# A depthwise stage's tables with memory of their own, made ready while x loads

## The chip, the cores and the metric

The kernel runs on one core of a Trainium2 chip. The metric is the device time of one execution in microseconds (us); the times given are medians over several executions.

## The reference, cut to what matters

x is [128, 256, 9, 9] in float32: 128 images, 256 channels, 81 pixels. One block is computed: a normalisation over channels, a convolutional attention, and a mixture of eight experts behind it. Cut to the parts around the change:

```python
xn = _ln_c(x)                                  # mean and variance over the 256 channels of each pixel
k  = xn.reshape(bs, c, hw).transpose(0, 2, 1)
k1 = conv1d(k, se_key_w, groups=hw) + se_key_b # 9 taps along the channels, a filter for each pixel
v  = conv2d(xn, se_val_w, groups=c) + se_val_b # 3x3 depthwise
k1s = relu(bn(conv2d(xn, sa_key_w, groups=c))) # 3x3 depthwise, with a batch norm folded in
out1 = band of softmax weights over v, + k1
out2 = k1s + softmax(...) * xn
x = x + alpha * out1 + (1 - alpha) * out2
x = x + experts(_ln_t(x))                      # top 2 of 8 experts on 10368 tokens
```

## The kernel before, in words

Five engines run programs of their own, written out by hand and joined by semaphores; SP issues nearly all DMAs, on one queue, in the order of its program. Two large buffers in on-chip memory, `big` and `pool_`, hold 128 partitions (images) by 20736 words each; a third, `aux`, has 4640 words. Parts of `pool_` and `aux` are handed out anew in each stage, by a cursor that is set back.

**Load and statistics.** SP issues the two halves of x into `big` (L264), twenty small weight loads (L273), and then one store from memory to memory that lays out the windows of the 1-D convolution, `u_d`, 81 x 128 rows of 544 bytes (L278); it waits for that. VectorE takes statistics of each pixel (L741, 60 pixels as two halves, 21 whole), with its sums after them (L756 to L763), one root on ScalarE (L1218) and a reciprocal (L731).

**Pixel stage, 27 turns of three pixels.** ScalarE normalises (L1226), POOL copies the result back to `big` (L1418), TensorE transposes (L426), VectorE copies the transposes to `xt_s` (L772), and TensorE convolves them with windows that SP loads from `u_d` into one of two buffers (L284, issued when the convolution of the turn before last is done); VectorE adds the bias and writes k1 over all of `pool_` (L781).

**Between the stages.** Once all of k1 is in `pool_`, its first columns must be stored to memory before the tables can lie there: SP stores words 0 to `tables_end` (5147) of 128 rows (L291) and waits; then it issues three small tables (L295: taps, batch norm and rows, 11 partitions each), the mask (L296: 75 partitions, 973 KB) and the rest of k1's first half (L297). VectorE meanwhile makes se_ab, sa_ab and alpha (L794 to L800), waits for the tables, folds the batch norm into the taps with a root on ScalarE (L804, L1240) and splits them into three bf16 parts (L803 to L816). Then it waits for the store of L297 and for POOL, and a memset of `pt_s` (L819) releases TensorE, POOL and ScalarE through `tab_c`.

**Depthwise stage, eight chunks of 32 channels.** VectorE copies the chunk's taps (L822). TensorE builds 82 x 162 matrices, one for each channel, as mask times taps (L475, nine groups of nine matmuls); ScalarE (L1248) and VectorE (L828) copy them in turn into `m_s`, which lies in `pool_` behind the tables. Then for eight quads of channels POOL copies xn (L1431), TensorE turns it (L459) and multiplies it by the matrices (L493), VectorE and ScalarE evict (L834, L1257, L1259), and SP stores v and ks (L310). The stores of xn (L302) and of k1's second half (L304) are issued between them.

Behind it come the attention stage, the router and the experts, which the change does not touch.

The lines that order the pause:

```python
            sp.wait_ge(S["k1_ev"], PIX_TURNS + CREDIT)
            sp.dma_start(k1_d[:, 0:tables_end], pool_[:, 0:tables_end]).then_inc(S["k1_out0"], 16)
            sp.wait_ge(S["k1_out0"], 16)
...
            dve.wait_ge(S["k1_outm"], 16)
            dve.wait_ge(S["xb_c"], PIX_TURNS + CREDIT)
            nc.vector.memset(pt_s[:, :, :, :], 1.0).then_inc(S["tab_c"], 1)
```

Of the kernel before, what the change touches and what calls it, by code (L numbers as in the profile page):

```python
# [4 lines left out]
BS, C, H, W = 128, 256, 9, 9  # L5
HW = H * W
# [6 lines left out]
BN_EPS, LN_C_EPS, LN_T_EPS = 1e-5, 1e-6, 1e-5  # L13
# [12 lines left out]
QUADS = C // QUAD  # L26
DEPTH = 4
CHUNK = 32
AUX = 4640
TAP_ROWS = 64 + 11  # L30
PIECE = 512
PIECES = EXPERTS * 4
# [18 lines left out]
def metaformer_kernel(nc, x, taps, tap_bn, tap_rows, toeplitz_mask, ident, band_masks, rot_masks, zstrings,  # L51
# [10 lines left out]
    fp32, fp16, bf16 = mybir.dt.float32, mybir.dt.float16, mybir.dt.bfloat16  # L62
    ALU, ACT, AX = mybir.AluOpType, mybir.ActivationFunctionType, mybir.AxisListType

    ctx = ExitStack()
    with ctx:
# [44 lines left out]
        cursor = [0]  # L111

        def take(parts, *dims):
            n = 1
            for d in dims:
                n *= d
            a = pool_[0:parts, cursor[0]:cursor[0] + n]
            cursor[0] += n
            assert cursor[0] <= C * HW
            names = "abcde"[:len(dims)]  # L120
            if len(dims) > 1:
                a = a.rearrange(f"p ({' '.join(names)}) -> p {' '.join(names)}",
                                **{m: d for m, d in zip(names, dims)})
            return a
# [23 lines left out]
        xt_s = take_aux(128, 2, PIX, C)  # L148
        kb_s = take_aux(128, HW)

        ps = ctx.enter_context(nc.psum_tensor("ps", [128, 8, 512], fp32))


        cursor[0] = 0
        bn_s = take(128, HW, 2 * HALVES, 3)

        cursor[0] = 0
        mask_s = take(TAP_ROWS, HW * (HW + 1) // 2).bitcast(bf16).rearrange("p (m n) -> p m n", n=HW + 1)
        taps_s = take(11, 2, C)
        tapr_s = take(11, 2, C)  # L160
        taph_s = take(TAP_ROWS, C).bitcast(bf16).rearrange("p (v c) -> p v c", v=2)
        tapc_s = take(TAP_ROWS, CHUNK).bitcast(bf16).rearrange("p (v c) -> p v c", v=2)
        tapbn_s = take(11, 2, C)
        taprow_s = take(11, 2)
        tables_end = cursor[0]
        m_s = take(HW + 1, CHUNK, 2, HW)
        assert cursor[0] <= C * HW // 2
        aux_at[0] = 0
        xq_s = take_aux(128, 2, QUAD, HW)
        pt_s = take_aux(HW + 1, 2, QUAD, BS)  # L170
# [89 lines left out]
        @block.sync  # L260
        def _(sp):
            half = C * HW // 2
            for h in range(HALVES):
                sp.dma_start(big[:, h * half:(h + 1) * half], x[:, h * half:(h + 1) * half]).then_inc(S[f"x_in{h}"], 16)  # L264
            n = 0
# [8 lines left out]
                n += 1  # L274
            assert 16 * n == W_IN

            window = bass.AP(zstrings.tensor, 127, [[ZLEN, HW], [-1, 128], [1, 136]])
            sp.dma_start(u_d, window).then_inc(S["win_out"], 16)  # L278
            sp.wait_ge(S["win_out"], 16)
# [8 lines left out]
                    load_bands(i * 2 + par, par)  # L288
            load_bands(PIX_TURNS - 1, 0)
            sp.wait_ge(S["k1_ev"], PIX_TURNS + CREDIT)  # L290
            sp.dma_start(k1_d[:, 0:tables_end], pool_[:, 0:tables_end]).then_inc(S["k1_out0"], 16)  # L291
            sp.wait_ge(S["k1_out0"], 16)

            for dst, src in ((taps_s, taps), (tapbn_s, tap_bn), (taprow_s, tap_rows)):
                sp.dma_start(dst, src).then_inc(S["tab_in"], 16)  # L295
            sp.dma_start(mask_s.bitcast(mybir.dt.uint16), toeplitz_mask).then_inc(S["mask_in"], 16)  # L296
            sp.dma_start(k1_d[:, tables_end:half], pool_[:, tables_end:half]).then_inc(S["k1_outm"], 16)  # L297
            sp.wait_ge(S["xb_c"], PIX_TURNS + CREDIT)
            with sp.Fori(0, QUADS // DEPTH) as i:

# [12 lines left out]
            for k in range(DEPTH):  # L313
                sp.wait_ge(S[f"st_v{k}"], 32 * (QUADS // DEPTH) + CREDIT)
            sp.wait_ge(S["xn_out"], 16 * (QUADS // DEPTH))
            sp.wait_ge(S["k1_out1"], 16 * (QUADS // DEPTH))

            def load_pair(i, first=False):
# [391 lines left out]
        def _(dve):  # L710
# [10 lines left out]
            def link(ins):  # L721

                start(ins)
                settled()
# [7 lines left out]

            early, unroll = 60, 15

            def pixel_statistics(first, pixels, run, chans, part):
# [56 lines left out]
            for p, ab in ((se_bn_s[:, :].unsqueeze(1), se_ab[:, :].unsqueeze(1)), (sa_bn_s, sa_ab)):  # L794
# [4 lines left out]
                link(nc.vector.tensor_tensor(ab[:, :, 1:2], bb, ab[:, :, 2:3], ALU.subtract))  # L799
            link(nc.vector.tensor_scalar(alpha_s[:, 1:2], alpha_s[:, 0:1], -1.0, 1.0, ALU.mult, ALU.add))  # L800

            dve.wait_ge(S["tab_in"], 48)
            link(nc.vector.memset(taph_s, 0.0))  # L803
            inverse_root(tapbn_s[:, 1, :], BN_EPS, 1.0, tapbn_s[:, 1, :])  # L804
            link(nc.vector.tensor_tensor(tapbn_s[:, 0, :], tapbn_s[:, 0, :], tapbn_s[:, 1, :], ALU.mult))
            link(nc.vector.tensor_scalar(tapbn_s[:, 0, :], tapbn_s[:, 0, :], taprow_s[:, 0:1], taprow_s[:, 1:2],
                                         ALU.mult, ALU.add))
            link(nc.vector.tensor_tensor(taps_s[:, 1, :], taps_s[:, 1, :], tapbn_s[:, 0, :], ALU.mult))


            for k in range(3):
                part = taph_s[32 * k:32 * k + 11]
                left = taps_s if k == 0 else tapr_s
                link(nc.vector.tensor_copy(part, left))
                if k < 2:
                    link(nc.vector.tensor_tensor(tapr_s, left, part, ALU.subtract))  # L816
            dve.wait_ge(S["k1_outm"], 16)
            dve.wait_ge(S["xb_c"], PIX_TURNS + CREDIT)
            nc.vector.memset(pt_s[:, :, :, :], 1.0).then_inc(S["tab_c"], 1)  # L819
            with dve.Fori(0, C // CHUNK) as i:  # L820
                dve.wait_ge(S["mb_p"], i * 9 + CREDIT)
                nc.vector.tensor_copy(tapc_s[:, :, :], taph_s[:, :, bass.ds(i * CHUNK, CHUNK)]).then_inc(S["tapc_c"], 1)  # L822
                for n in range(1, 9, 2):
                    dve.wait_ge(S["mb_p"], i * 9 + n + 1 + CREDIT)
                    if n == 1:
                        dve.wait_ge(S["cv_p"], i * 8 + CREDIT)
                    flat = ps[0:HW + 1, 2:4, :].rearrange("p b n -> p (b n)")[:, 0:9 * 2 * CHUNK]
                    nc.vector.tensor_copy(m_s[:, :, :, n * 9:(n + 1) * 9].rearrange("p c v m -> p m v c"),  # L828
                                          flat.rearrange("p (m v c) -> p m v c", m=9, v=2)).then_inc(S["mb_e1"], 1)
                for k in range(CHUNK // QUAD):  # L830
                    q, par = i * (CHUNK // QUAD) + k, k % 2
                    dve.wait_ge(S["tq_p"], q + 1 + CREDIT)
                    dve.wait_ge(S["cv_p"], q - 1 + CREDIT)
                    nc.vector.tensor_copy(pt_s[0:HW, par, :, :].rearrange("p c b -> p (c b)"),  # L834
                                          ps[0:HW, 4 + par, :]).then_inc(S["pt_c"], 1)
# [379 lines left out]
        @block.scalar  # L1215
        def _(act):
            act.wait_ge(S["var_c"], 1)
            nc.scalar.activation(stats[:, 1, :], stats[:, 1, :], ACT.Sqrt).then_inc(S["root_c"], 1)  # L1218

            def normalise(i, par):  # L1220
# [12 lines left out]
                    normalise(i * 2 + par, par)  # L1233
            normalise(PIX_TURNS - 1, 0)
            for n, v in enumerate((se_ab[:, 0:1], sa_ab[:, :, 0:1])):
                act.wait_ge(S["var_c"], n + 2)
                nc.scalar.activation(v, v, ACT.Sqrt).then_inc(S["root_c"], 1)

            act.wait_ge(S["var_c"], 4)
            nc.scalar.activation(tapbn_s[:, 1, :], tapbn_s[:, 1, :], ACT.Sqrt).then_inc(S["root_c"], 1)  # L1240
            act.wait_ge(S["tab_c"], 1)
            with act.Fori(0, C // CHUNK) as i:
                for n in range(0, 9, 2):
                    act.wait_ge(S["mb_p"], i * 9 + n + 1 + CREDIT)
# [332 lines left out]
```

## Time and profile before

| | |
|---|---|
| time, three runs | 1769.7, 1773.2, 1778.4 us (median 1773.2) |
| the profiled execution, its own time | 1770.6 us |
| its span, first to last instruction | 1768.9 us |
| TensorE matmul busy | 1377.7 us (78%) |
| VectorE busy | 1140.3 us (64%) |
| ScalarE busy | 802.4 us (45%) |
| GpSimd busy | 650.0 us (37%) |
| moved by DMA | 250.5 MB |

In the rows, PE is TensorE's matmuls, PEld its weight loads, DVE VectorE, ACT ScalarE, POOL GpSimd, SP SyncE; SPq is SP's sequencer, which issues the DMAs. L with a number is a line of the kernel. Busy times of overlapping engines do not add up to the span; idle time of an engine costs only where the chain of waits runs through it.

### The profile page before, as it was taken

How to read it: one execution, taken by the hardware profiler on the slowest of the kernel's cores; microseconds unless marked ns; L12 is line 12 of the kernel's file. 1: busy time of each engine (PE TensorE's matmuls, PEld its weight loads, DVE VectorE, ACT ScalarE, POOL GpSimd, SP SyncE). 2: the span in 40 equal slices, each digit the busy share in tenths (PEclk: the TensorE clock that was granted, in tenths of full speed). 3: DMA queues.
4: the chain of work that ended last, by engine and by line, in shares of the span. 5: the costliest groups of instructions: out<-in, count | busy, mean ns of one | idle time of the engine just before them, and what ended most of it. 6: DMA issues, size and time to landing. Idle time of an engine off the chain costs nothing.

```text
span 1768.9 us, 38225 instructions
## 1 busy us (share of the span) xinstructions
PE 1377.7 (78%) x9764; PEld 1124.1 (64%) x9765; DVE 1140.3 (64%) x3074; ACT 802.4 (45%) x1779; POOL 650.0 (37%) x561
## 2 busy tenths in 40 slices
PE   0393988979999999999755555399999999999300
PEld 0383888955666666666555555288888888888300
DVE  6894343326767666676478888566666666666493
ACT  0491444435434344444299999233333333333250
POOL 0260111114333333333056767354544545445200
PEclk9995888879999999999555555699999999999755
DMA  8534435468666666765133333432323223332485
GB/s 300 122 91 170 183 149 194 166 188 190 159 169 155 160 162 153 173 150 142 50 99 122 125 122 123 144 92 81 95 85 94 85 88 92 87 94 76 177 317 240
DMA packets 259222, 250.50 MB, mean 142 GB/s; under 512 B 150089, under 2 KB 234398, under 8 KB 255156
## 3 DMA queue, kind: packets, MB, share of 16 engines
q1 hardware_dynamic: 238879, 196.95, 38.0%
q0 software_dynamic: 20320, 53.28, 9.1%
q8 instruction: 9, 0.15, 0.0%
q14 instruction: 14, 0.11, 0.0%
HBM read 152.07 MB, written 105.57 MB: 146 GB/s over the span
## 4 chain that ended last, share of the span: by engine, by line
PE 68%; DVE 12%; ACT 7%; DMA 6%; issue 4%; SPq 1%; DVEq 1%; ACTq 0%; POOLq 0%; POOL 0%
PE ps L686 14%; PE ps L671 13%; PE ps L510 6%; PE ps L493 5%; PE ps L459 4%; PE ps L565 3%; PE ps L537 3%; PE ps L561 3%; ACT pool_ L1248 2%; PE ps L520 2%; PE ps L655 2%; DVE big L1205 2%; PE ps L529 2%; PE ps L563 2%; DMA aux<-u_d 2%
## 5 line engine op out<-in xcount | busy, mean ns | idle before, releaser
L1475 POOL DMA_INDIRECT y_d<-pool_,to_s x176 | 254.8, 1447 | 282.8 <-DVE pool_ L1165 246.8
L686 PE MATMUL ps<-pool_,aux 128*128 x2112 | 249.6, 274 | 5.2 <-DVE aux L1157 3.4
L671 PE MATMUL ps<-aux,pool_ 128*128 128x256 f16 x2112 | 246.8, 274 | 1.0 <-ACT aux L1376 0.6
L686 PEld LDWEIGHTS ps<-pool_,aux 128*128 128x128 f16 x2112 | 198.4, 98 | 50.5 <-issue 23.5
L671 PEld LDWEIGHTS ps<-aux,pool_ 128*128 x2112 | 206.5, 98 | 25.9 <-issue 1.6
L1376 ACT ACTIVATE aux<-ps,b_s 128x256 f32<-128x256 f32 x352 | 138.0, 474 | 162.2 <-DVE aux L1157 162.0
L1455 POOL DMA_INDIRECT rows_d<-aux,idx_s x162 | 160.2, 989 | 108.3 <-DVE idx_s L1068 58.9
L1165 DVE SCALAR_TENSOR_TENSOR pool_<-ps,pool_ 128x512 f32<-128x512 f32 x88 | 60.9, 692 | 140.0 <-PE ps L686 140.0
L1447 POOL DMA_DIRECT2D pool_<-v_d x64 | 50.0, 781 | 272.4 <-PE ps L567 271.0
L1368 ACT ACTIVATE aux<-ps 128x512 f16<-128x512 f32 x88 | 52.6, 597 | 172.7 <-PE ps L655 172.7
L510 PE MATMUL ps<-pool_,se_w_s 81*81 81x512 f32 x256 | 118.7, 607 | 5.6 <-DMA pool_<-k_d 5.6
L1283 ACT ACTIVATE pool_<-ps,sa_ab 128x324 f32<-128x324 f32 x64 | 39.7, 621 | 159.7 <-PE ps L522 159.7
L1157 DVE TENSOR_TENSOR aux<-aux 128x1024 f16<-128x1024 f32 x88 | 107.8, 1225 | 3.1
L1431 POOL COPY aux<-big 128x324 f32 x64 | 29.2, 457 | 215.6 <-PE ps L459 186.3
L834 DVE COPY aux<-ps 81x512 f32<-81x512 f32 x64 | 43.9, 686 | 87.5 <-PE ps L459 87.5
L459 PE MATMUL ps<-ident_s,aux 128*81 128x128 f32 x512 | 77.9, 302 | 25.7 <-POOL aux L1431 25.7
L1295 ACT ACTIVATE pool_<-ps,pool_ 128x81 f32<-128x81 f32 x256 | 79.5, 336 | 29.2 <-DVE pool_ L865 29.2
L855 DVE TENSOR_REDUCE pool_<-ps 128x4 f32<-128x324 f32 x64 | 31.6, 496 | 93.5 <-PE ps L529 91.9
L493 PE MATMUL ps<-pool_,aux 82*128 82x162 f32 x512 | 90.5, 326 | 0.0
L459 PEld LDWEIGHTS ps<-ident_s,aux 128*81 128x81 f32 x512 | 70.7, 173 | 25.9 <-POOL aux L1431 25.9
L493 PEld LDWEIGHTS ps<-pool_,aux 82*128 82x128 f32 x512 | 81.4, 209 | 0.6
L426 PE MATMUL ps<-ident_s,aux 128*128 128x128 f32 x162 | 23.5, 284 | 70.6 <-ACT aux L1226 70.6
(202 smaller groups left out, 3079.2 us busy)
## 6 DMA issues: line engine op xcount, KB each, us to landing
pool_<-rows_d SPq DMA_DIRECT2D x88, 258.0 KB
pool_<-y_d SPq DMA_DIRECT2D x18, 1152.0 KB, 8.7
big<-in_x SPq DMA_DIRECT2D x2, 5184.0 KB, 21.0
xn_d<-big SPq DMA_DIRECT2D x16, 648.0 KB, 3.0
v_d<-aux SPq DMA_DIRECT2D x64, 162.0 KB, 1.9
ks_d<-aux SPq DMA_DIRECT2D x64, 162.0 KB, 2.0
pool_<-xn_d SPq DMA_DIRECT2D x32, 324.0 KB
pool_<-k_d SPq DMA_DIRECT2D x32, 324.0 KB
```

The source lines that it names most:

```text
L459: last = nc.tensor.matmul(ps[0:HW, 4 + par, c * BS:(c + 1) * BS], xq_s[:, par, c, :], ident_s[:, :], start=True, stop=True)
L493: last = nc.tensor.matmul(o, pt_s[:, par, c, :], m_s[:, k * QUAD + c, :, :] .rearrange("p v n -> p (v n)"), start=True, stop=True)
L510: last = nc.tensor.matmul(ps[0:HW, n, :], se_w1_s[:, k, :], kq_s[:, par, k, 2 * n:2 * n + 2, :].rearrange("p b j -> p (b j)"), start=k == ...
L537: last = nc.tensor.matmul(ps[:, 2, TOK + j * D:TOK + (j + 1) * D], a_s[:, par, j // 2, (j % 2) * 128:(j % 2 + 1) * 128], se_w2_s[:, :], st ...
L671: last = nc.tensor.matmul(o, w_s[:, a, bass.ds(e * (4 * PIECE) + (k * HID + j * 128), 128)], xh_s[:, par, b, k * SLOTS:(k + 1) * SLOTS], s ...
L686: last = nc.tensor.matmul(ps[:, 6 + par, s * C:(s + 1) * C], hh_s[:, par, a, j, s * 128:(s + 1) * 128], w_s[:, b, bass.ds(e * (4 * PIECE) ...
L1157: nc.vector.tensor_tensor(lo, hf_s, hi, ALU.subtract).then_inc(S["hlo_c"], 1)
L1165: nc.vector.scalar_tensor_tensor(yo_s[:, par], ps[:, 6 + par, :].rearrange("p (s c) -> p s c", s=2), 1.0 / WSCALE, b2_s[:, bass.ds(e * C, ...
L1295: ins = nc.scalar.activation(e_s[:, par, h, b, :], ps[:, 2 + h, b * HW:(b + 1) * HW], ACT.Exp, bias=sm_s[:, par, 2, j:j + 1], accum_out=sm ...
L1376: nc.scalar.activation(hf_s[:, j * SLOTS:(j + 1) * SLOTS], ps[:, 2 + 2 * par + j // 2, (j % 2) * SLOTS:(j % 2 + 1) * SLOTS], ACT.Gelu, bia ...
L1455: nc.gpsimd.indirect_dma_start(out=rows_d[:, :], out_offset=bass.IndirectOffsetOnAxis(ap=idx_s[:, slot, k:k + 1], axis=0), in_=xf_s[:, slo ...
L1475: nc.gpsimd.indirect_dma_start(out=y_d[:, :], out_offset=bass.IndirectOffsetOnAxis(ap=to_s[:, par, k:k + 1], axis=0), in_=yo_s[:, par, k, ...
```

## The change

The mask (`mask_s`), the split taps (`taph_s`) and a chunk's taps (`tapc_s`) move from `pool_` to the end of `aux`, which grows from 4640 to 7904 words. The tables that the split reads go to the second half of `pool_`. SP issues the three tables ahead of x, and the mask between the weights and the window store. VectorE folds and splits the taps ahead of its statistics; ScalarE's root for it comes first. The matrices `m_s` now begin at word 0 of `pool_`. SP stores their 5184 words of rows 0 to 95 first, then those of rows 96 to 127, then the rest of the half, with no wait between; VectorE's and ScalarE's first matrix copies wait for the store of 96 rows, the memset no longer waits for a store.

```diff
--- before.py
+++ after.py
@@ -26,7 +26,7 @@
 QUADS = C // QUAD
 DEPTH = 4
 CHUNK = 32
-AUX = 4640
+AUX = 7904
 TAP_ROWS = 64 + 11
 PIECE = 512
 PIECES = EXPERTS * 4
@@ -148,23 +148,27 @@
         xt_s = take_aux(128, 2, PIX, C)
         kb_s = take_aux(128, HW)

+        mask_s = take_aux(TAP_ROWS, HW * (HW + 1) // 2).bitcast(bf16).rearrange("p (m n) -> p m n", n=HW + 1)
+        taph_s = take_aux(TAP_ROWS, C).bitcast(bf16).rearrange("p (v c) -> p v c", v=2)
+        tapc_s = take_aux(TAP_ROWS, CHUNK).bitcast(bf16).rearrange("p (v c) -> p v c", v=2)
         ps = ctx.enter_context(nc.psum_tensor("ps", [128, 8, 512], fp32))


         cursor[0] = 0
         bn_s = take(128, HW, 2 * HALVES, 3)

-        cursor[0] = 0
-        mask_s = take(TAP_ROWS, HW * (HW + 1) // 2).bitcast(bf16).rearrange("p (m n) -> p m n", n=HW + 1)
+        cursor[0] = C * HW // 2
         taps_s = take(11, 2, C)
         tapr_s = take(11, 2, C)
-        taph_s = take(TAP_ROWS, C).bitcast(bf16).rearrange("p (v c) -> p v c", v=2)
-        tapc_s = take(TAP_ROWS, CHUNK).bitcast(bf16).rearrange("p (v c) -> p v c", v=2)
         tapbn_s = take(11, 2, C)
         taprow_s = take(11, 2)
-        tables_end = cursor[0]
+        cursor[0] = 0
         m_s = take(HW + 1, CHUNK, 2, HW)
-        assert cursor[0] <= C * HW // 2
+        m_end = cursor[0]
+        m_rows = 96
         aux_at[0] = 0
         xq_s = take_aux(128, 2, QUAD, HW)
         pt_s = take_aux(HW + 1, 2, QUAD, BS)
@@ -260,6 +264,8 @@
         @block.sync
         def _(sp):
             half = C * HW // 2
+            for dst, src in ((taps_s, taps), (tapbn_s, tap_bn), (taprow_s, tap_rows)):
+                sp.dma_start(dst, src).then_inc(S["tab_in"], 16)
             for h in range(HALVES):
                 sp.dma_start(big[:, h * half:(h + 1) * half], x[:, h * half:(h + 1) * half]).then_inc(S[f"x_in{h}"], 16)
             n = 0
@@ -274,6 +280,7 @@
                 n += 1
             assert 16 * n == W_IN

+            sp.dma_start(mask_s.bitcast(mybir.dt.uint16), toeplitz_mask).then_inc(S["mask_in"], 16)
             window = bass.AP(zstrings.tensor, 127, [[ZLEN, HW], [-1, 128], [1, 136]])
             sp.dma_start(u_d, window).then_inc(S["win_out"], 16)
             sp.wait_ge(S["win_out"], 16)
@@ -288,13 +295,9 @@
                     load_bands(i * 2 + par, par)
             load_bands(PIX_TURNS - 1, 0)
             sp.wait_ge(S["k1_ev"], PIX_TURNS + CREDIT)
-            sp.dma_start(k1_d[:, 0:tables_end], pool_[:, 0:tables_end]).then_inc(S["k1_out0"], 16)
-            sp.wait_ge(S["k1_out0"], 16)
-
-            for dst, src in ((taps_s, taps), (tapbn_s, tap_bn), (taprow_s, tap_rows)):
-                sp.dma_start(dst, src).then_inc(S["tab_in"], 16)
-            sp.dma_start(mask_s.bitcast(mybir.dt.uint16), toeplitz_mask).then_inc(S["mask_in"], 16)
-            sp.dma_start(k1_d[:, tables_end:half], pool_[:, tables_end:half]).then_inc(S["k1_outm"], 16)
+            sp.dma_start(k1_d[0:m_rows, 0:m_end], pool_[0:m_rows, 0:m_end]).then_inc(S["k1_out0"], 16)
+            sp.dma_start(k1_d[m_rows:BS, 0:m_end], pool_[m_rows:BS, 0:m_end]).then_inc(S["k1_outm"], 16)
+            sp.dma_start(k1_d[:, m_end:half], pool_[:, m_end:half]).then_inc(S["k1_outm"], 16)
             sp.wait_ge(S["xb_c"], PIX_TURNS + CREDIT)
             with sp.Fori(0, QUADS // DEPTH) as i:

@@ -313,6 +316,7 @@
             for k in range(DEPTH):
                 sp.wait_ge(S[f"st_v{k}"], 32 * (QUADS // DEPTH) + CREDIT)
             sp.wait_ge(S["xn_out"], 16 * (QUADS // DEPTH))
+            sp.wait_ge(S["k1_outm"], 32)
             sp.wait_ge(S["k1_out1"], 16 * (QUADS // DEPTH))

             def load_pair(i, first=False):
@@ -732,6 +736,22 @@

+            dve.wait_ge(S["tab_in"], 48)
+            link(nc.vector.memset(taph_s, 0.0))
+            inverse_root(tapbn_s[:, 1, :], BN_EPS, 1.0, tapbn_s[:, 1, :])
+            link(nc.vector.tensor_tensor(tapbn_s[:, 0, :], tapbn_s[:, 0, :], tapbn_s[:, 1, :], ALU.mult))
+            link(nc.vector.tensor_scalar(tapbn_s[:, 0, :], tapbn_s[:, 0, :], taprow_s[:, 0:1], taprow_s[:, 1:2],
+                                         ALU.mult, ALU.add))
+            link(nc.vector.tensor_tensor(taps_s[:, 1, :], taps_s[:, 1, :], tapbn_s[:, 0, :], ALU.mult))
+            for k in range(3):
+                part = taph_s[32 * k:32 * k + 11]
+                left = taps_s if k == 0 else tapr_s
+                link(nc.vector.tensor_copy(part, left))
+                if k < 2:
+                    link(nc.vector.tensor_tensor(tapr_s, left, part, ALU.subtract))
             early, unroll = 60, 15

             def pixel_statistics(first, pixels, run, chans, part):
@@ -799,22 +819,6 @@
                 link(nc.vector.tensor_tensor(ab[:, :, 1:2], bb, ab[:, :, 2:3], ALU.subtract))
             link(nc.vector.tensor_scalar(alpha_s[:, 1:2], alpha_s[:, 0:1], -1.0, 1.0, ALU.mult, ALU.add))

-            dve.wait_ge(S["tab_in"], 48)
-            link(nc.vector.memset(taph_s, 0.0))
-            inverse_root(tapbn_s[:, 1, :], BN_EPS, 1.0, tapbn_s[:, 1, :])
-            link(nc.vector.tensor_tensor(tapbn_s[:, 0, :], tapbn_s[:, 0, :], tapbn_s[:, 1, :], ALU.mult))
-            link(nc.vector.tensor_scalar(tapbn_s[:, 0, :], tapbn_s[:, 0, :], taprow_s[:, 0:1], taprow_s[:, 1:2],
-                                         ALU.mult, ALU.add))
-            link(nc.vector.tensor_tensor(taps_s[:, 1, :], taps_s[:, 1, :], tapbn_s[:, 0, :], ALU.mult))
-
-
-            for k in range(3):
-                part = taph_s[32 * k:32 * k + 11]
-                left = taps_s if k == 0 else tapr_s
-                link(nc.vector.tensor_copy(part, left))
-                if k < 2:
-                    link(nc.vector.tensor_tensor(tapr_s, left, part, ALU.subtract))
-            dve.wait_ge(S["k1_outm"], 16)
             dve.wait_ge(S["xb_c"], PIX_TURNS + CREDIT)
             nc.vector.memset(pt_s[:, :, :, :], 1.0).then_inc(S["tab_c"], 1)
             with dve.Fori(0, C // CHUNK) as i:
@@ -822,6 +826,8 @@
                 nc.vector.tensor_copy(tapc_s[:, :, :], taph_s[:, :, bass.ds(i * CHUNK, CHUNK)]).then_inc(S["tapc_c"], 1)
                 for n in range(1, 9, 2):
                     dve.wait_ge(S["mb_p"], i * 9 + n + 1 + CREDIT)
+                    if n == 1:
+                        dve.wait_ge(S["k1_out0"], 16)
                     if n == 1:
                         dve.wait_ge(S["cv_p"], i * 8 + CREDIT)
                     flat = ps[0:HW + 1, 2:4, :].rearrange("p b n -> p (b n)")[:, 0:9 * 2 * CHUNK]
@@ -1215,6 +1221,8 @@
         @block.scalar
         def _(act):
             act.wait_ge(S["var_c"], 1)
+            nc.scalar.activation(tapbn_s[:, 1, :], tapbn_s[:, 1, :], ACT.Sqrt).then_inc(S["root_c"], 1)
+            act.wait_ge(S["var_c"], 2)
             nc.scalar.activation(stats[:, 1, :], stats[:, 1, :], ACT.Sqrt).then_inc(S["root_c"], 1)

             def normalise(i, par):
@@ -1233,12 +1241,11 @@
                     normalise(i * 2 + par, par)
             normalise(PIX_TURNS - 1, 0)
             for n, v in enumerate((se_ab[:, 0:1], sa_ab[:, :, 0:1])):
-                act.wait_ge(S["var_c"], n + 2)
+                act.wait_ge(S["var_c"], n + 3)
                 nc.scalar.activation(v, v, ACT.Sqrt).then_inc(S["root_c"], 1)

-            act.wait_ge(S["var_c"], 4)
-            nc.scalar.activation(tapbn_s[:, 1, :], tapbn_s[:, 1, :], ACT.Sqrt).then_inc(S["root_c"], 1)
             act.wait_ge(S["tab_c"], 1)
+            act.wait_ge(S["k1_out0"], 16)
             with act.Fori(0, C // CHUNK) as i:
                 for n in range(0, 9, 2):
                     act.wait_ge(S["mb_p"], i * 9 + n + 1 + CREDIT)
```

## Rows read from the trace of the kernel before

**Rows 1.** The page's part 4: the chain that ended last, by line.
```profile
PE ps L686 14%; PE ps L671 13%; PE ps L510 6%; PE ps L493 5%; PE ps L459 4%; PE ps L565 3%; PE ps L537 3%; PE ps L561 3%; ACT pool_ L1248 2%; PE ps L520 2%; PE ps L655 2%; DVE big L1205 2%; PE ps L529 2%; PE ps L563 2%; DMA aux<-u_d 2%
```

**Rows 2.** Stage table: busy us by engine, granted clock, DMA share, GB/s.
```profile
core 0: us, PE busy (x) PEld busy (x) DVE busy (x) ACT busy (x) POOL busy (x), PEclk, DMA share, GB/s
137.00:161.00 24.00, 0.00 (x0) 0.00 (x0) 8.73 (x25) 0.82 (x3) 0.37 (x1) 0.56 0.83 306
```

**Rows 3.** Chain of waits, 128 to 230 us: start, us, what.
```profile
137.06 7.59 DMA k_d<-pool_
...
146.22 12.76 DMA k_d<-pool_
...
163.87 1.26 ACT pool_ L1248
```

**Rows 4.** Timeline, 128 to 190 us, VectorE: start, us, instruction, idle before and releaser.
```profile
139.32 0.15 DVE L800 TENSOR_SCALAR alpha_s<-alpha_s 128x1 f32<-128x1 f32 x1
...
147.05 0.27 DVE L803 MEMSET pool_<- 75x256 uint32 x1 [7.58 <-DMA pool_<-in_tap_rows]
...
153.57 0.42 DVE L814 CAST pool_<-pool_ 11x512 bf16<-11x512 f32 x1
159.29 0.91 DVE L819 MEMSET aux<- 82x1024 f32 x1 [5.30 <-DMA k_d<-pool_]
```

**Rows 5.** Timeline, 0 to 100 us, SP's issues, VectorE and TensorE.
```profile
0.84 0.86 SPq L264 DMA_DIRECT2D big<-in_x  x2
...
16.25 44.63 DVE L741 BATCH_NORM_STATS2 pool_<-big  x141 [16.12 <-DMA big<-in_x]
...
31.45 1.01 SPq L278 DMA_DIRECT2D u_d<-in_zstrings  x1
...
70.41 29.12 SPq L284 DMA_DIRECT2D aux<-u_d  x13
...
72.16 1.54 PE L426 MATMUL ps<-ident_s,aux 128*128 128x128 f32 x6 [0.62 <-ACT aux L1226]
...
73.49 0.78 PE L437 MATMUL ps<-aux 128*128 128x132 f32 x2
```

**Rows 6.** Chain of waits, 60 to 130 us: a window load.
```profile
76.12 2.69 DMA aux<-u_d
```

**Rows 7.** DMA issues by line: count, KB each, median us to landing.
```profile
big<-in_x SPq DMA_DIRECT2D x2, 5184.0 KB, 21.0
...
aux<-u_d SPq DMA_DIRECT2D x27, 204.0 KB, 2.6
...
k_d<-pool_ SPq DMA_DIRECT2D x1, 2573.5 KB, 7.6
...
pool_<-in_toeplitz_mask SPq DMA_DIRECT2D x1, 972.9 KB, 7.2
```

**Rows 8.** Stage table: window store, mask and second k1 store under way.
```profile
38.00:40.00 2.00, 0.00 (x0) 0.00 (x0) 2.00 (x9) 0.00 (x0) 0.00 (x0) 1.00 0.67 164
...
150.00:151.00 1.00, 0.00 (x0) 0.00 (x0) 0.93 (x3) 0.00 (x0) 0.00 (x0) 0.50 0.87 207
...
155.00:156.00 1.00, 0.00 (x0) 0.00 (x0) 0.00 (x0) 0.00 (x0) 0.00 (x0) 0.50 1.08 464
```

**Rows 9.** Stage table: granted clock 5 us after the last matmul.
```profile
140.00:141.00 1.00, 0.00 (x0) 0.00 (x0) 0.00 (x0) 0.00 (x0) 0.00 (x0) 0.55 0.77 329
```

**Rows 10.** Chain of waits, 128 to 230 us: matmuls and transposes of one quad.
```profile
174.30 2.23 PE ps L493 x8
...
185.97 1.11 PE ps L493 x8
187.08 0.88 PE ps L459 x8
```

**Rows 11.** Timeline, 160 to 400 us: VectorE's tap copy that begins a chunk.
```profile
188.63 0.18 DVE L822 COPY pool_<-pool_ 75x64 bf16 x1
217.74 0.18 DVE L822 COPY pool_<-pool_ 75x64 bf16 x1
244.15 0.17 DVE L822 COPY pool_<-pool_ 75x64 bf16 x1
```

## The prediction, made before the changed kernel was run

> **What bounds the kernel now.** I read the page's chain first. TensorE heads it with the two expert matmul lines, and the pixel stage's window loads have 2% [rows 1]: no engine's share tells what this change is worth, so I went to the two places that it touches. The table of stages shows the larger one: from 137 to 161 us TensorE does nothing, VectorE has 8.7 us of work, and the DMA engines are 83% busy [rows 2]. The chain there says why [rows 3]: the last k1 column is in at 137.06; the first store of k1 takes 7.59 us and SP waits for it; 1.6 us go to issuing tables and mask; the second store then takes 12.76 us, and VectorE stands before its memset (L819) until 159.29. The matrices' first copy by ScalarE (L1248) starts at 163.87. Beside that, VectorE ends its small constants at 139.47 and idles until the tables are in at 147.05, where its tap split runs 6.94 us, to 153.99 [rows 4]. The split is thus covered by the second store, and moving it alone is worth nothing.
>
> The other place is the start. SP issues x at 0.84, the window store at 31.45 and, once that has landed, the first window load at 70.41. The statistics run without a gap from 16.25 to 60.88; the first convolution starts at 73.49, right behind the second group of transposes [rows 5]. From there every second turn waits for a window load, issued when the convolution before last is done: 2.69 us, then the convolution [rows 6]. What delays the first load delays all 27 turns by as much.
>
> **The change, part by part.** All times are those of the profiled execution: span 1768.9, own time 1770.6; the median of the runs is 1773.2, 2.6 above it. A measurement of this kernel can tell about 0.5%, 8.9 us, from no change.
>
> *The pause.* Removed from the path: the wait for the whole store, the issue of tables and mask, the second store, the split. VectorE reaches the memset right behind its last constant, at 139.5 (POOL's copies back to big went turn by turn, and I count them done). The same steps as before follow: memset, POOL's copy, TensorE's first quad, nine mask matmuls, together 163.87 − 159.29 = 4.58 us from memset to first copy [rows 3, 4], so that copy could start at 144.1. It now waits for the 96-row store as well. That one is issued at 137.06 and is three quarters of a store that took 7.59 us [rows 3, 7]: by bytes, with 1.6 us of it fixed (estimated from the 1.6 us between the last table's issue and its landing, [rows 4]), 6.1 us, so there would be nothing to wait for. The nearest row for a transfer with fewer than 128 rows speaks against bytes: the mask, 75 rows, moved at 207 GB/s with the engines 87% busy, where a store of 128 rows went at 464 GB/s [rows 8], and its 0.97 MB took 7.2 us to land [rows 7]. So I take the full 7.6 us: landed at 144.65, and the first copy at 144.75. The upper bound is the 12.8 us of the store that had the mask ahead and others behind: 149.9. Gain: 163.87 − 144.75 = 19.1 us (bounds 19.8 and 14.0).
>
> A rule of the Trainium skill bears on this, "SBUF — State Buffer", section "Door 1: The DMA port swizzle": partitions 0 to 63 reach only eight of the sixteen ports. By it 96 rows last as long as 128 and the gain is 19.1; by bytes alone it would be 19.8. The mask's row agrees with the rule.
>
> The clock was granted at half (1.2 of 2.4 GHz) within 5 us of the last matmul [rows 9]; with matmuls resuming at 141.4 instead of 161.1 it has fallen too, so the first chunk is priced as it is. The rest of k1's first half, then xn and the first part of the second half, follow on the same queue: 6.3 MB in all, at 464 GB/s 13.6 us, over near 151, before the first v store is due. Waits in the loops that are already met I count at nothing: the semaphore is full from the first chunk on.
>
> *The split at the start.* Three tables are issued ahead of x. At 0.43 us each (two issues of x took 0.86 [rows 5]) x starts 1.3 us later and lands at 17.4 instead of 16.1. Tables land some 1.6 us after their issue, so at 3.6; the split's 6.94 us end at 10.5. Cover: x's load, 6.9 us of it spare; without that each us would count. ScalarE's root lies in the 6.94. Price on VectorE's chain 1.3 us, and the same for everything that SP issues later.
>
> *The mask ahead of the window store.* Here the change gives back. The mask's issue puts another 0.4 us before the window store, and its packets stand in front of that store's in the same queue. It landed after 7.2 us [rows 7]; without some 2 us of start and landing, the engines have it for 5 to 5.5 us. If the window store's packets had room beside it, the cost would be nil: that store ran with 67% of the engines busy. But the mask kept them 87% busy for only 207 GB/s [rows 8], so I take them one after the other. The window store starts 1.3 + 0.4 + 5 = 6.7 us later, less some 0.4 where the issue overlaps: 6.3; it is bound by its own 10,368 rows of 544 bytes, so it ends as much later. The first load was issued at 70.41 and takes 2.6 [rows 5, 7], so it was in at 73.0 to 73.1, 0.4 us before it was needed: 5.9. The first convolution and the step to the next load took 73.49 to 76.12 on its slow first matmuls and may win up to 1 us with its inputs all there; I take 0.4 off. **5.5 us later.** Bounds: 1.3 (the mask wholly beside the rest, VectorE's chain alone) and 1.3 + 0.4 + 7.2 − 0.3 = 8.6.
>
> *Sum:* −19.1 + 5.5 = −13.6 us: 1770.6 becomes 1757.0, and at the level of the median 1759.6. I say 1759.
>
> **The rivals.** *A, the mask is hidden* (chance 0.17): the window store leaves a third of the engines' time free, and 1 MB is little beside 38 us of it. Against: the queue is one, and the mask stands in front. Gain 19.1 − 1.3 = 17.8: 1755.5.
>
> *B, the first store lands late* (0.12): two more stores, 3.3 MB, and then xn are issued right behind it without a wait. The row for it is the second store, 12.8 us for 2.6 MB with neighbours; against it, x's halves landed one after the other (the first in by 16.1, the median of the two 21.0 [rows 5, 7]), so the queue keeps its order well. First copy at 149.9: 14.0 − 5.5 = 8.5: 1764.7, at the border of no change.
>
> *C, the granted clock* (0.09, of which 0.03 slower). Place: each of the eight chunks. It begins at the half clock, which rises in its dense half, at times sooner, at times later: from 188.63 to 217.74 a chunk took 29.1 us, the next 26.4 [rows 11]. If the shift puts six more chunks at the price of the first, some 2 us each, 12 us go: 1771.2, the same. Price at the worst: eight matmuls of L493 took 2.23 us at the half clock, 1.11 at the full one, and eight transposes 0.88 at the full one [rows 10], so if the rise never comes inside a chunk, its eight quads cost 8 × (1.12 + 0.88) = 16 us more, less some 3 already paid: 8 × 13 = 104, and the time is some 1863, slower. It decides from 13.6 + 8.9 = 22.5 us over the eight chunks, 2.8 us each. Against: the code of a chunk is unchanged, and nothing makes TensorE's work in it thinner.
>
> *D, the wait is not gone* (0.04): the tables land only when x has, whose rows of 41 KB follow in the same queue. x's halves land at 17.4 and, by the median of the two, at 28.3; then the split ends at 35.2, the statistics start 19 us late, and all is given back: 1773. It decides from tables landing after 10.5. Against: they are issued first and are 45 KB.
>
> **How the numbers follow.** Forecast as worked, 0.58: faster by over 0.5%. A, 0.17: faster. B, 0.12: around the border, 0.07 faster, 0.05 same. C, 0.09: 0.06 same, 0.03 slower. D, 0.04: 0.03 same, 0.01 slower. Together faster 0.82, same 0.14, slower 0.04. The range goes from A with the first chunks losing some 4 us less on the clock than they did, 1773.2 − 17.8 − 4 = 1751.4, to B with the mask at its upper bound, 1773.2 − (14.0 − 8.6) = 1767.8.
>
> **What would show it.** In the changed kernel: the split between 3.6 and 11 us, statistics from 17.5; the first window load issued at 76 to 77 and the first convolution at 79; k1 in at 142.6; the memset at 145; the 96-row store landing 7.6 us after its issue; ScalarE's first copy 7.7 us after k1 is in, instead of 26.8; chunks of 27 to 29 us behind it. It is wrong if the first window load is issued before 74 (A), if that first copy waits for the store by over 3 us (B), if the chunks together last over 8 us longer (C), or if the statistics start after 20 (D).

## The result, and the profile after

| | before | changed |
|---|---|---|
| median of 5 runs | 1773.2 us | 1761.4 us (1759.0 to 1763.4) |
| ratio, 95% interval | | 0.9921 [0.9898, 0.9945] |
| profiled execution, own time | 1770.6 us | 1759.0 us |
| its span | 1768.9 us | 1757.3 us |

The kernel is faster by 0.8%, 11.6 us between the two spans. The forecast was 1759, within 1751 to 1768. Measured twice more beside other kernels, the changed kernel stood at 0.9924 [0.9909, 0.9938] and 0.9936 [0.9918, 0.9953] of the kernel before, 13.2 and 12.4 us between the medians.

The span of each falls into four stretches whose edges are rows: k1 in (issue of its first store), first matrix copy by ScalarE, last chunk's tap copy, end.

| stretch | before | changed | difference |
|---|---|---|---|
| start to k1 in | 137.06 | 144.00 | +6.94 |
| k1 in to first copy | 26.81 | 9.21 | −17.60 |
| first copy to last chunk's tap copy | 188.93 | 187.73 | −1.20 |
| from there to the end | 1416.1 | 1416.4 | +0.3 |

The change touches the first two stretches. Together they gave back 10.7 us; the last 0.9 of the 11.6 lie in stretches that it does not touch.

The timeline of the changed kernel, 0 to 85 us, answers to [rows 5] (columns as there):

```profile
3.24 0.27 DVE L740 MEMSET aux<- 75x256 uint32 x1 [3.11 <-DMA pool_<-in_tap_rows]
...
9.74 0.42 DVE L751 CAST aux<-pool_ 11x512 bf16<-11x512 f32 x1
17.98 44.62 DVE L761 BATCH_NORM_STATS2 pool_<-big  x141 [7.82 <-DMA big<-in_x]
...
32.95 0.44 SPq L283 DMA_DIRECT2D aux<-in_toeplitz_mask  x1
33.43 1.01 SPq L285 DMA_DIRECT2D u_d<-in_zstrings  x1
...
73.86 1.54 PE L430 MATMUL ps<-ident_s,aux 128*128 128x128 f32 x6 [0.62 <-ACT aux L1234]
```

The split runs from 3.24 to 10.16 and VectorE then idles 7.82 us, waiting for x: the split is free here. The window store is issued 2.0 us later than before. Its landing shows in the chain of waits, 60 to 100 us (start, us, what), which answers to [rows 6]:

```profile
33.43 42.17 DMA u_d<-in_zstrings
...
75.97 2.64 DMA aux<-u_d
...
78.83 0.81 PE ps L441 x2
79.64 0.44 PE ps L443 x2
...
81.84 1.28 PE ps L430 x6
...
84.29 0.23 PE ps L443 x2
...
94.12 0.66 PE ps L430 x6
```

The chain now runs through the store itself, for 42.2 us; before, from 31.45 to 70.05, it took 38.6. The first convolution comes at 78.83, 5.3 us later, and it waits for the window load, no longer for the transposes. A pair of its matmuls takes 0.44 us, twice the 0.23 of later, and they stay slow until 84.0, where before they were quick from 75.3 on. TensorE had stood from 75.4 to 78.83, but it had not been quick before that either: six transposes (L430) took 1.54 us at 73.86, and on the chain six take 1.28 us at 81.84 and 0.66 at 94.12. The stage table prints a granted clock of 1.00 over all of this. That is a gap and not a reading: the trace's first record of the granted clock is the one of full speed that begins at 84.0 in this trace and at 75.3 in the one before, and where there is no record the table prints 1.00. The durations and the first record agree.

The pause, in the timeline of 142 to 154 us, answers to [rows 3, 4]:

```profile
144.00 0.36 SPq L298 DMA_DIRECT2D k_d<-pool_  x1
...
146.27 0.15 DVE L820 TENSOR_SCALAR alpha_s<-alpha_s 128x1 f32<-128x1 f32 x1
146.69 0.91 DVE L823 MEMSET aux<- 82x1024 f32 x1 [0.28 <-DVE alpha_s L820]
...
148.54 2.00 PE L463 MATMUL ps<-ident_s,aux 128*81 128x128 f32 x8 [6.12 <-POOL aux L1438]
...
153.09 1.23 DVE L834 COPY pool_<-ps 82x576 f32<-82x576 f32 x1 [5.45 <-DMA k_d<-pool_]
153.21 1.24 ACT L1255 ACTIVATE pool_<-ps 82x576 f32<-82x576 f32 x1 [7.77 <-DMA k_d<-pool_]
```

The memset stands right behind VectorE's constants, and both first copies wait for the store of 96 rows. The DMA issues by line (count, KB each, us to landing) answer to [rows 7]:

```profile
k_d<-pool_ SPq DMA_DIRECT2D x1, 2592.0 KB, 19.6
...
k_d<-pool_ SPq DMA_DIRECT2D x1, 1944.0 KB, 8.9
...
aux<-in_toeplitz_mask SPq DMA_DIRECT2D x1, 972.9 KB, 7.5
k_d<-pool_ SPq DMA_DIRECT2D x1, 648.0 KB, 13.9
```

The 96-row store has a quarter fewer bytes than the store before and needs 1.3 us more from issue to landing, 8.9 for 7.6. The rest of the half takes 19.6 us, and nobody waits for it.

### The profile page after: what moved, and what is told of

It is laid out like the page before. It is cut to its first block, busy times and chain, and to the rows that moved or that the text cites. A ratio compares the mean times of both kernels' runs of the same rounds, so it can differ in the third digit from the quotient of the medians.

```text
span 1757.3 us, 38235 instructions
## 1 busy us (share of the span) xinstructions
PE 1375.9 (78%) x9764; PEld 1122.8 (64%) x9765; DVE 1140.7 (65%) x3074; ACT 802.5 (46%) x1779; POOL 649.3 (37%) x561
## 4 chain that ended last, share of the span: by engine, by line
PE 68%; DVE 11%; ACT 7%; DMA 6%; issue 3%; SPq 3%; DVEq 0%; ACTq 0%; POOLq 0%; POOL 0%
PE ps L690 14%; PE ps L675 13%; PE ps L514 6%; PE ps L497 5%; PE ps L463 4%; PE ps L541 3%; PE ps L569 3%; PE ps L565 2%; DMA u_d<-in_zstrings 2%; ACT pool_ L1255 2%; PE ps L524 2%; PE ps L659 2%; DVE big L1211 2%; PE ps L533 2%; PE ps L567 2%
## 5 line engine op out<-in xcount | busy, mean ns | idle before, releaser
L675 PEld LDWEIGHTS ps<-aux,pool_ 128*128 x2112 | 206.3, 98 | 25.4 <-issue 1.5
L430 PE MATMUL ps<-ident_s,aux 128*128 128x128 f32 x162 | 24.2, 290 | 72.3 <-ACT aux L1234 72.3
L1425 POOL COPY big<-aux 128x768 f32 (+1 forms) x27 | 42.1, 1557 | 95.6 <-ACT aux L1234 95.6
```

The source lines that it names most:

```text
L675: last = nc.tensor.matmul(o, w_s[:, a, bass.ds(e * (4 * PIECE) + (k * HID + j * 128), 128)], xh_s[:, par, b, k * SLOTS:(k + 1) * SLOTS], s ...
```

## The experiments

Each is the changed kernel with one edit. A single span of this kernel moves by some us in stretches that no edit touches: over all kernels here the one from first copy to the last chunk's tap copy took 186.8 to 190.8 us, the one behind it 1416 to 1424. The first of these follows TensorE's clock: in the fourteen traces the granted clock was at half for 73.2 to 78.7 us of it, least where the stretch was shortest and most where it was longest. So edits of a few us are read from the stretch they touch. The first four kernels were run once each, and so was the kernel before, at 1775.6.

**The wait restored.** Tables and mask stay early, but the memset waits for all of k1's first half:

```diff
+            dve.wait_ge(S["k1_outm"], 32)
             dve.wait_ge(S["xb_c"], PIX_TURNS + CREDIT)
             nc.vector.memset(pt_s[:, :, :, :], 1.0).then_inc(S["tab_c"], 1)
```

> The changed kernel, but VectorE's memset waits for all of k1's first half again, as in the kernel before; tables and mask stay early. Theory (the gain of the change is the wait, not the split or the mask): the last of the three stores landed 19.6 us after its issue in the changed kernel, so the memset comes near 164.5 and the first copy near 169, 25 us after k1 is in: 16 us slower than the changed kernel, 1775. Rival (the early tables and mask brought the gain): under 5 us slower.

1777.4 us, and the timeline shows VectorE before the memset:

```profile
142.74 0.36 SPq L298 DMA_DIRECT2D k_d<-pool_  x1
...
163.58 0.91 DVE L824 MEMSET aux<- 82x1024 f32 x1 [18.43 <-DMA k_d<-pool_]
...
168.17 1.25 ACT L1256 ACTIVATE pool_<-ps 82x576 f32<-82x576 f32 x1 [24.00 <-PE ps L479]
```

25.4 us from k1 in to the first copy, as expected, against 26.8 in the kernel before: of the 17.6 us that the change took out of this stretch, 16.2 are back, and the whole advantage over the kernel before is gone. The gain is the wait; the early tables and mask only make it possible.

**The split behind the pixel stage again.** The tables need memory of their own for it, in aux:

```diff
-            dve.wait_ge(S["tab_in"], 48)
-            link(nc.vector.memset(taph_s, 0.0))
...
             link(nc.vector.tensor_scalar(alpha_s[:, 1:2], alpha_s[:, 0:1], -1.0, 1.0, ALU.mult, ALU.add))
+            dve.wait_ge(S["tab_in"], 48)
+            link(nc.vector.memset(taph_s, 0.0))
...
```

> The changed kernel, but the tables lie in aux and VectorE folds and splits the taps behind the pixel stage again, between its constants and the memset. Theory (the split had to move because the store that covered it is gone): its 6.9 us now stand on the path behind k1, the memset 6.9 us later than in the changed kernel, the first matrix copy about 11.6 + 2.5 = 14.1 us after k1 is in instead of 9.2, the kernel 4.9 us slower than the changed one. Rival (the store of 96 rows covers it still): first copy 9.2 us after k1, no difference.

k1 was in at 142.81 and the first copy came at 157.12, released by TensorE and not by the store:

```profile
152.53 0.91 DVE L822 MEMSET aux<- 82x1024 f32 x1 [0.28 <-DVE aux L816]
...
157.12 1.25 ACT L1254 ACTIVATE pool_<-ps 82x576 f32<-82x576 f32 x1 [10.74 <-PE ps L478]
```

14.3 us for 9.2: without its cover the split costs 5.1 of its 6.9 us, the rest being the time that the store takes anyway. Here the copy comes 4.59 us behind the memset, with no store in its way. 1766.6 us.

**The neighbours held back.**

```diff
             sp.dma_start(k1_d[0:m_rows, 0:m_end], pool_[0:m_rows, 0:m_end]).then_inc(S["k1_out0"], 16)
+            sp.wait_ge(S["k1_out0"], 16)
             sp.dma_start(k1_d[m_rows:BS, 0:m_end], pool_[m_rows:BS, 0:m_end]).then_inc(S["k1_outm"], 16)
```

> The changed kernel, but SP waits for the store of 96 rows before it issues the next stores. Theory (the neighbours behind it in the queue slow it): it lands after 7.6 us instead of 8.9 and the first matrix copy comes 7.9 us after k1, a gain of 1.3 us. Rival (96 rows are slow by themselves, through the rows that they lie in): it lands after 8.9 us as before and nothing moves. Rival (bytes alone): 6.1 us, the first copy then bound by the mask matmuls, 7.1 us after k1.

```profile
k_d<-pool_ SPq DMA_DIRECT2D x1, 1944.0 KB, 8.8
```

8.8 us with nothing behind it, the first copy 9.1 us after k1. So the neighbours are not the cause. That it is not the bytes either, but the rows that the store takes, the next runs show. The whole took 1764.3 us, which says nothing: the copy's gain is 0.1 us, the stretch behind the chunks was 1423.

**All 128 rows in one store.**

```diff
-        m_rows = 96
+        m_rows = BS
...
-            sp.dma_start(k1_d[m_rows:BS, 0:m_end], pool_[m_rows:BS, 0:m_end]).then_inc(S["k1_outm"], 16)
...
-            sp.wait_ge(S["k1_outm"], 32)
+            sp.wait_ge(S["k1_outm"], 16)
```

> The changed kernel, but one store takes all 128 rows of the matrices' words and the first copies wait for it; the store of 32 rows goes. Theory (the 96 rows are held up by the rows 0 to 63 and their neighbours, not by their number): it lands after the same 8.9 us, within 0.5. Rival (bytes count): 8.9 us grow by a third of the part that is not fixed, to 11.3 us, and the first copy comes 2.4 us later. Rival (the split store costs a fixed part of its own): it lands earlier, 7.6 us, as the whole store did before.

The chain of waits, 142 to 182 us:

```profile
142.03 7.64 DMA k_d<-pool_
...
149.99 1.25 ACT pool_ L1254
```

A third more bytes land 1.2 us earlier, after 7.6 us, as the whole store did before the change. The first copy comes 7.96 us behind k1, right behind the store, and VectorE's first copy waits for TensorE. The kernel ran at 1766.1 us, with 1424 in the stretch behind the chunks. The expectation's last rival gave this time. The stage tables of the two, in 1 us steps, show how the rows went (last column GB/s, the one before it the DMA engines' busy share). A row of 20.7 KB counts whole, with its bytes and its time, in the step in which it starts: 332 GB/s are sixteen rows, 664 are two waves of sixteen and no rate of the engines, and a share can exceed 1. Held back, 96 rows:

```profile
145.00:146.00 1.00, 0.00 (x0) 0.00 (x0) 0.89 (x2) 0.00 (x0) 0.00 (x0) 0.50 0.57 187
146.00:147.00 1.00, 0.21 (x1) 0.21 (x2) 0.00 (x0) 0.00 (x0) 0.72 (x2) 0.50 1.11 353
147.00:148.00 1.00, 1.00 (x6) 1.00 (x6) 0.00 (x0) 0.00 (x0) 0.13 (x1) 0.50 0.84 311
148.00:149.00 1.00, 1.00 (x10) 0.98 (x9) 0.00 (x0) 0.00 (x0) 0.00 (x0) 0.50 0.71 270
149.00:150.00 1.00, 1.00 (x15) 0.89 (x13) 0.00 (x0) 0.00 (x0) 0.46 (x1) 0.50 0.31 99
```

128 rows in one:

```profile
144.00:145.00 1.00, 0.00 (x0) 0.00 (x0) 0.66 (x4) 0.00 (x0) 0.00 (x0) 0.50 0.80 332
145.00:146.00 1.00, 0.00 (x0) 0.00 (x0) 0.67 (x2) 0.00 (x0) 0.00 (x0) 0.50 0.77 332
146.00:147.00 1.00, 0.43 (x2) 0.43 (x3) 0.00 (x0) 0.00 (x0) 0.86 (x2) 0.50 1.56 664
147.00:148.00 1.00, 1.00 (x7) 1.00 (x6) 0.00 (x0) 0.00 (x0) 0.00 (x0) 0.50 0.77 332
148.00:149.00 1.00, 1.00 (x13) 0.98 (x12) 0.00 (x0) 0.00 (x0) 0.18 (x1) 0.50 0.77 332
```

The 96 rows run unevenly and thin out at the end; the 128 run in even waves. The trace's records of single rows say the same more sharply. Each of the 128 rows took 0.77 to 0.81 us, and the sixteen parts of the store's completion came within 0.2 us, 7.44 to 7.65 behind the issue. Of the 96 rows, held back, 31 took 1.2 to 1.9 us and the others mostly 0.8, and the parts came from 6.3 to 8.8. The first row starts 0.86 to 0.87 us behind the issue in both, and the rows' times add up to about the same, 98.9 us for 96 and 100.3 for 128. So the expectation's reason, a fixed part for the split, is not what happened: the lost time lies in single slow rows. What makes those rows slow these records do not show.

**112 rows**, the same line with 112, run once later (the kernel before then stood at 1773.9, median of eleven):

> The changed kernel with 112 rows in the first store instead of 96 (7 for each of 16 engines instead of 6). 128 rows landed in 7.6 us, 96 in 8.8 to 8.9. Theory (any share of the rows that leaves the ports uneven is slow): it lands after 8.5 to 9 us, or longer. Rival (only 96 is a bad number): 7 to 7.6 us, the first copy 8.0 us behind k1.

```profile
k_d<-pool_ SPq DMA_DIRECT2D x1, 2268.0 KB, 9.0
```

9.0 us, the first copy 9.3 us behind k1, the kernel 1765.3 us. Both stores with fewer than 128 rows are slower than the one with all of them.

The other kernels were timed in two groups of five or six executions each, with the changed kernel in each group. The first group:

> The changed kernel once more, beside the kernels of this call on the same chip: 1761, 12 us under the kernel before, k1 in at 144.0.

0.9924 [0.9909, 0.9938], 1756.2 us against 1769.4 of the kernel before; k1 in at 142.4, 1.6 earlier than in the first profile. The statistics on x started at 17.4 instead of 18.0, the first window load was issued at 75.06, and the stretch from first convolution to k1 in took 64.4 us instead of 65.2.

**The mask right behind x.**

```diff
             for h in range(HALVES):
                 sp.dma_start(big[:, h * half:(h + 1) * half], x[:, h * half:(h + 1) * half]).then_inc(S[f"x_in{h}"], 16)
+            sp.dma_start(mask_s.bitcast(mybir.dt.uint16), toeplitz_mask).then_inc(S["mask_in"], 16)
             n = 0
...
-            sp.dma_start(mask_s.bitcast(mybir.dt.uint16), toeplitz_mask).then_inc(S["mask_in"], 16)
```

> The changed kernel, but SP issues the mask right behind x, ahead of the twenty weights, so that it is through before the window store. Theory (the mask's packets held the window store up by about 5 us): the first window load is issued near 71.3 instead of 76.0, the first convolution comes at 75.5, bound by VectorE's chain, without the cold first turns; k1 is in near 139, 5 us earlier, the kernel 5 us faster, 1756. Rival (the queue holds the same bytes, so the window store ends when it ended): nothing moves. Rival (the mask makes SP hang longer on the full queue): the weights and the window store come 5 us later and all is given back.

0.9931 [0.9915, 0.9946]: nothing gained, and k1 in at 143.3, 0.9 us later than in the changed kernel of the group. The timeline of SP's issues (the second number is how long SP stood in the issue):

```profile
6.20 23.18 SPq L280 DMA_DIRECT2D se_bn_s<-in_se_bn  x1
...
30.94 2.80 SPq L280 DMA_DIRECT2D sa_b_s<-in_sa_b  x1
...
37.81 1.01 SPq L285 DMA_DIRECT2D u_d<-in_zstrings  x1
76.34 1.09 SPq L291 DMA_DIRECT2D aux<-u_d  x2
```

The window store itself took 38.2 us from issue to landing, as before the change (38.6), so the mask in front of it was what made it 42. But SP stood longer in its issues (23.2 us in one where it had been 21.0, and 2.8 in another) and issued it 4.7 us later than in the changed kernel of the group. This is the expectation's second rival.

**The window store right behind x**, the weights and the mask after it:

```diff
             for h in range(HALVES):
                 sp.dma_start(big[:, h * half:(h + 1) * half], x[:, h * half:(h + 1) * half]).then_inc(S[f"x_in{h}"], 16)
+            window = bass.AP(zstrings.tensor, 127, [[ZLEN, HW], [-1, 128], [1, 136]])
+            sp.dma_start(u_d, window).then_inc(S["win_out"], 16)
             n = 0
             for dst, src in ((ident_s[:, :], ident), (band_s[:, :], band_masks), (rot_s[:, :], rot_masks),
...
-            window = bass.AP(zstrings.tensor, 127, [[ZLEN, HW], [-1, 128], [1, 136]])
-            sp.dma_start(u_d, window).then_inc(S["win_out"], 16)
```

> The changed kernel, but the window store is issued right behind x, ahead of weights and mask. Theory (the store is bound by its own small rows and only needs an early place): it is done near 66, before VectorE's chain; the first convolution at 75.5, k1 in near 139, 5 us faster than the changed kernel, 1756. Rival (the weights now land behind it, and transposes and convolutions wait for them): they are in after 70, and each us later costs one; if the mask is behind them too, nothing is gained over the changed kernel.

0.9930 [0.9917, 0.9944]. SP's issues:

```profile
4.01 57.05 SPq L281 DMA_DIRECT2D ident_s<-in_ident  x1
...
69.43 0.44 SPq L285 DMA_DIRECT2D aux<-in_toeplitz_mask  x1
70.27 1.08 SPq L291 DMA_DIRECT2D aux<-u_d  x2
```

The store has landed at 65.1, as expected. But SP stands in one issue for 57 us and needs another 8 for the small loads; the first window load, issued 0.8 us behind the mask, takes 6.5 us and is in only at 76.8, and the first convolution comes at 77.03. k1 is in at 140.80, 1.6 us before the changed kernel of the group, not 3.4.

**Both, with the later stores held back**: the edits of that run and of the held neighbours together.

> The window store behind x as in the run before, and SP holds the later k1 stores back until the store of 96 rows has landed. If both theories hold, 5 and 1.3 us add up: 1755, 6.3 us under the changed kernel. Rival: the held stores end later and delay the first v stores, and the 1.3 us come back.

0.9919 [0.9905, 0.9934], 1754.8 us; k1 in at 141.19, first copy 9.1 us behind it. That is 1.4 us under the changed kernel where 6.3 were expected, and not to be told from it. The second group:

> The changed kernel again, as the measure for the two kernels of this call that change the mask's queue: 0.992 to 0.993 of the kernel before, k1 in between 142 and 144.

0.9936 [0.9918, 0.9953], 1761.5 us against 1773.9 of the kernel before; k1 in at 142.50.

**The mask from ScalarE's queue**, once x is in:

```diff
-            sp.dma_start(mask_s.bitcast(mybir.dt.uint16), toeplitz_mask).then_inc(S["mask_in"], 16)
...
+            act.wait_ge(S["x_in1"], 16)
+            nc.scalar.dma_start(mask_s.bitcast(mybir.dt.uint16), toeplitz_mask).then_inc(S["mask_in"], 16)
             act.wait_ge(S["var_c"], 2)
             nc.scalar.activation(stats[:, 1, :], stats[:, 1, :], ACT.Sqrt).then_inc(S["root_c"], 1)
```

> The changed kernel, but ScalarE issues the mask on its own queue as soon as the second half of x is in (about 28 us), while SP still issues small weights. Theory (what costs is the mask in front of the window store in one queue, and ahead of the weights it makes SP hang): the mask lands near 35, the window store is issued at 32.6 and nearly undelayed, the first window load comes near 71.5 and the first convolution near 75, k1 is in near 139.5, 3 to 4 us before the changed kernel of this call. Rival (the engines have the same bytes to move before the window store, whatever the queue): the first window load is issued at 75 again and nothing moves.

The mask is issued at 29.33 and lands after 7.4 us. The chain of waits, 60 to 90 us:

```profile
32.74 40.37 DMA u_d<-in_zstrings
73.48 2.80 DMA aux<-u_d
76.50 0.80 PE ps L440 x2
```

The window store takes 40.4 us: half of what the mask cost it is left. The mask lands at 36.7 and the store is issued at 32.7, so the two still overlap. k1 is in at 140.49, 2.0 us before the changed kernel of the group, where 3 to 4 were expected. 0.9920 [0.9904, 0.9936] against 0.9936 for the changed kernel: the intervals overlap.

**That, with 128 rows.**

> As the run before, and the first k1 store takes 128 rows in one, as e4 did. If both hold: 3 to 4 us from the window store and 1.2 us from the first copy (8.0 us behind k1 instead of 9.2), 5 us in all under the changed kernel, 0.989 to 0.990 of the kernel before. Rival: the granted clock of the first chunk rises at a time that does not move with it, and up to 2 us come back there.

k1 in at 141.34, first copy 7.97 us behind it, 149.31: 2.4 us before the changed kernel's 151.71. The kernel stood at 0.9934 [0.9917, 0.9952], not at the 0.989 to 0.990 that was expected. The store's 1.2 us are all there, of the mask's 3 to 4 only 1.2, and in the whole time neither shows: 2.4 us are 0.14%, and these intervals are 0.3% wide. No version here is shown to beat the changed kernel.

## Why the prediction was right

*The direction and the size.* Forecast −13.6 us, measured −11.6 between the spans and −11.8 between the medians. The term that decided was read from one stretch, 137 to 164 us [rows 2, 3], and the restored wait showed that 16.2 of its 17.6 us are the wait. That the total came within 2 us is in part luck. The pause gave 17.6 us where 19.1 were forecast, the start cost 6.9 where 5.5 were, so the two came to −10.7 (−12.3 and −12.2 in the two profiles that followed), and stretches that the change does not touch moved by −0.9.

*The pause: right, one term short.* The 4.58 us from memset to first copy held: 4.59 where the late split left the store out of the way. In the changed kernel they end at 146.69 + 4.58 = 151.27, which is 7.3 us behind k1 in, where 7.0 was reckoned (144.1 − 137.06); the copy itself waited for the store until 153.2. The step that was too small is the landing of the store: "So I take the full 7.6 us". It took 8.9. The argument chose between bytes (6.1) and the mask's row, and took the length of the whole store as the most that three quarters of it could need. The run with 128 rows shows that fewer rows can last longer than all. The port rule of "SBUF — State Buffer" (section "Door 1: The DMA port swizzle") in the Trainium skill gives equal times for 96 and 128 rows; measured are 8.8 and 7.6, so it has the direction against bytes right and not the amount. Rival B named the right term with the wrong mechanism: holding the neighbours back gave 0.1 us. The stores behind it, which nobody waits for, were reckoned at 464 GB/s; that figure is one 1 us step with a share of 1.08 [rows 8], and they were not over 14 us behind k1 in: the rest of the first half alone landed 20.5 us behind it.

*The split: right.* Tables in at 3.2 (3.6 reckoned), split done at 10.2 (10.5), 7.8 us of cover left. x came 1.7 us later in the first profile, 1.1 to 1.2 in the two that followed; reckoned 1.3.

*The mask ahead of the window store: right in kind, sized by two errors that cancel only in part.* The first window load was due 6.3 us later and came 5.6 later: the mask lengthened the store by 3.6 us instead of the 5 assumed, and the issues took 2.0 instead of 1.7. So the two do overlap in part, as rival A held; it fell as a whole, since 3.6 of 5 us remained. The first convolution was due 5.9 us later and came 5.3 later. Then "may win up to 1 us with its inputs all there; I take 0.4 off" was wrong in sign. From first convolution to k1 in it took 65.2 us instead of 63.6, so k1 was in 6.9 us later and not 5.5. In the other two profiles of the same kernel that stretch was 64.4 and 64.0: the price is 0.4 to 1.6 us. TensorE's slow start goes with it: by the first record of full clock it ran slowly for 1.8 us behind the first convolution before the change, and for 5.2, 5.9 and 3.1 us in these three profiles. The slow time and the price do not grow in step (5.9 us at a price of 0.8), and the stop ahead of it was longest, 3.6 us, where the price was least, so how the 1.6 us arise stays open.

*The granted clock (C)* was at half for 74.2 us of the stretch with the chunks, 75.2 before, and the stretch moved by −1.2 us; over all kernels it took 186.8 to 190.8. It is the noise of these comparisons and not a cost of the change. *D* fell at once: the tables landed before x.

## What to carry to other kernels

When a stage starts behind a store, ask which words of it the stage overwrites and wait for those alone, and move into earlier loads whatever the old wait had covered; here the second only pays with the first. A load moved "for free" stands in front of something in its queue: look at what is issued right behind it, and at how long the issuing engine already stands in its issues there. Do not cut rows off a transfer to make it faster before having timed both shapes.

## What the runs showed that I had not expected

A store of 96 or 112 of 128 rows, each row 20.7 KB, landed after 8.8 to 9.0 us, one of 128 rows after 7.6. The time is lost in single rows, which took up to 1.9 us where all of 128 took 0.8. How rows are dealt to the engines is in no row that I read, so the cause stays open; that neighbours in the queue are not the cause is shown.

SP can hang in one small issue when large transfers stand ahead of it in its queue: 20 to 21 us behind x, 23 with the mask there too, 57 with the window store, after which each small load still costs its 0.4 us. That the queue is full then is my reading of this; no row shows it. An early place in the queue for a large transfer is paid by all small ones behind it.

A granted clock of 1.00 in a stage table can mean that there is no record. TensorE's matmuls ran at half speed from its first transposes to 84.0 us (a pair of L441 in 0.44 us, later 0.23) while the table printed 1.00; the trace's first clock record begins at 84.0.
